# Causal masking of the first four query tiles' diagonal blocks: by TensorE in PSUM, or by ScalarE and GpSimd in SBUF

## The chip, the cores and the metric

The kernel runs on one core of one Trainium2 chip. The metric is the device time of one execution in microseconds, the median of several runs. Engines are named as in the profile: PE is TensorE (PEld its weight loads), DVE is VectorE, ACT is ScalarE, POOL is GpSimd, SP issues most DMAs.

## The reference

One transformer layer with adaptive modulation, in float32, on x of shape (16, 1024, 256):

```python
h = layernorm(x) * (1 + ca) + sa
x = x + ga * attn(h)        # attn: layer norm, Wq/Wk/Wv, rope, causal softmax, Wo; 16 heads of 16
h = layernorm(x) * (1 + cb) + sb
x = x + gb * moe_ffn(h)     # 8 experts, 512 tokens each, gathered and added back by index

scores = q @ k.T / 4        # attention, per batch and head
scores = scores * mask + (1 - mask) * -1e9      # mask: lower triangle
out = softmax(scores) @ v
```

The change lies in the attention alone. The exact maximum of each row of masked scores is taken there ahead of the exponentials.

## The kernel before, in words

Five phases follow each other: modulation vectors and weights (0), layer norms, q, k and v (1), attention (2), output projection (3) and the experts (4). The change is in phase 2. Its scores are products of bfloat16 parts: q and k are split into three parts each, six products of which are stacked on 96 rows, so that one pass gives a float32-like score.

A **unit** is one batch and one group of HG = 4 heads: 16 x 4 = 64 units. A row of 1024 queries is cut into T = 8 query tiles of 128. Each unit needs two passes over its scores:

- The pass for the **maxima** (`fill`, `largest`) has queries on the partitions. It goes through 20 slots (`SLOTS`, s0 to s19), each of two PSUM banks with up to 1024 score columns; even and odd slots take turns on two pairs of banks. TensorE fills a slot in two halves (`FILLS`, 40 of them), VectorE takes the row maxima of it in one reduction (line 946). Where a slot holds diagonal blocks, TensorE adds the causal mask by one more product of a unit matrix with `mask_b` (line 1034). Slot 4 (`TURN`) is kept free: there the finished maxima of the unit before are turned by TensorE (`turn_max`) and negated and split by VectorE (`negate`), then split on by GpSimd (`parts`) and sent by two DMAs of SP through DRAM (`maxima`) into rows 96 to 98 of q.
- The pass for the **exponentials** (`scores_for_exp`, `exp`, `weigh`) has keys on the partitions. It goes through NPC = 10 pieces of 4 heads each. For each head TensorE writes up to 512 columns into one of three banks (line 1052), with the negated maximum added by the three extra rows; ScalarE takes the exponential (line 992); GpSimd clears the upper triangle of diagonal blocks (line 885); two pieces later TensorE multiplies with v (`weigh`, line 1071). ScalarE copies the two halves of the output out of PSUM ahead of pieces 2 and 5 (`copy_out`, line 980).

Each engine's order is written out by hand. TensorE runs, for unit u and each of its 40 score matmuls n (piece n // 4, head n % 4), the score for the exponential and then fill n of unit u + 2; so piece i carries slots 2i and 2i + 1 of the unit two ahead. After four heads comes `weigh`. A fill of slot s waits until the slot s - 2, on the same banks, is reduced (line 1024); a score waits until the exponential three heads earlier is done (line 1050). VectorE goes through the slots in order. The last two units have nothing to fill ahead; the first two are filled in a prologue with no scores between.

Widths of the pieces: 0 has 512 columns a head, 1 has 384 + 128, 2 has 256, 3 to 7 have 512, 8 has 384 + 128, 9 has 256. Slots before: s0 has the diagonal blocks of tiles 0 and 4, s1 tile 1, s2 and s3 tile 2, s5 and s6 tile 3, s7 to s14 the first 512 columns of tiles 4 to 7, s15 to s19 the rest of tiles 5 to 7.

Of the kernel before, what the change touches and what calls it, by code (L numbers as in the profile page):

```python
# [17 lines left out]
F32 = mybir.dt.float32  # L18
# [3 lines left out]
ALU = mybir.AluOpType  # L22
ACT = mybir.ActivationFunctionType
AX = mybir.AxisListType
# [692 lines left out]
def phase2(nc, B, L, ps, ident, mask, q_d, k_d, v_d, max_d, att_d):  # L717
# [25 lines left out]
    both_banks = lambda i, k0, w: [[[(h, i, 0, k0, w)], [(h + 1, i, 0, k0, w)]] for h in range(0, HG, 2)]  # L743
    four = lambda i, k0: [(h, i, h * P, k0, P) for h in range(HG)]
    pairs = lambda i, k0: [[(h, i, (h % 2) * 256, k0, 256) for h in (n, n + 1)] for n in range(0, HG, 2)]
    SLOTS = [[four(0, 0), four(4, HALF)], pairs(1, 0)]
    for i in (2, 3):
        SLOTS += both_banks(i, 0, (i + 1) * P)
    for i in range(4, T):
        SLOTS += both_banks(i, 0, HALF)  # L750
    SLOTS += [pairs(5, HALF)]
    for i in (6, 7):
        SLOTS += both_banks(i, HALF, (i - 3) * P)
    TURN = 4
    SLOTS.insert(TURN, None)
    NS = len(SLOTS)
    NR = NS - 1
    real = lambda s: s - (s > TURN)
    FILLS = []
    for s, slot in enumerate(SLOTS):  # L760
        FILLS += [(s, 0), (s, 1)]
# [7 lines left out]
    with ExitStack() as ctx:  # L769
# [6 lines left out]
        prob = sb("prob", [P, RING, HG, 512], F32)  # L776
        unit_b = sb("unit_b", [P, P], BF16)
        mask_b = sb("mask_b", [P, P], BF16)
        mx = sb("mx", [P, 2, HG, T], F32)
        mx0 = sb("mx0", [P, 2, HG, 4], F32)  # L780
        m_rest = sb("m_rest", [HG * T, 2, P], F32)
# [1 line left out]
        o_sb = sb("o_sb", [P, 2, HALF], F32)  # L783

        qk_in, v_in, m_in = many("p2_qk_in", UNITS), many("p2_v_in", UNITS), many("p2_m_in", UNITS)
        ones_set, consts = sem("p2_ones_set"), sem("p2_consts")
        a_ready, a_free = sem("p2_a_ready"), sem("p2_a_free")
        turned = sem("p2_turned")
        max_done = sem("p2_max_done")
# [87 lines left out]
        @block.gpsimd  # L877
        def _(pool):
            def select(un, i):
                b, g, u = un  # L880

                wait_apart(pool, exp_done, u * NEXP + (i + 1) * HG)
                for _, at, _, _ in PIECES[i][1]:
                    own = prob[:, (g * NPC + i) % RING, :, at:at + P]
                    pool.affine_select(out=own, in_=own, compare_op=ALU.is_ge, fill=0.0, base=0,  # L885
                                       pattern=[[0, HG], [1, P]], channel_multiplier=-1).then_inc(sel_done, 1)

            def parts(un):

                b, g, u = un  # L890
                rest = m_rest[:, g % 2, :]
                wait_apart(pool, m_left, u + 1)
                pool.tensor_copy(m3[:, g % 2, 1, :], rest).then_inc(m_mid, 1)
                pool.wait_ge(m_mid, u + 1)
                pool.tensor_tensor(m3[:, g % 2, 2, :], rest, m3[:, g % 2, 1, :], ALU.subtract).then_inc(m_parts, 1)

            def step(un, ahead):
                for i in range(NPC):
                    if diag(PIECES[i]):
                        select(un, i)  # L900
                    if i == 3 and ahead is not None:
                        parts(prior(ahead))
                if ahead is None and un[1] == NG - AHEAD:
                    parts(unit(LAST, NG - 1))

            def prologue():
                for g in range(NG):
                    pool.memset(k[ROWS:P, g], 1.0).then_inc(ones_set, 1)
                parts(unit(0, 0))

            steps(pool, prologue, step)

        @block.vector
        def _(dve):
            def finish(un):
                b, g, u = un
                dve.wait_ge(a_free, u * NR + NR)
                late = mx[:, g % 2, :, 4:8]
                dve.tensor_tensor(late, late, mx0[:, g % 2], ALU.max).then_inc(max_done, 1)

            def negate(un):

                b, g, u = un
                hi, src = m3[:, g % 2, 0, :], ps[0:HG * T, PS_A + 2 * (TURN % 2), 0:P]
                dve.wait_ge(turned, u + 1)
                reuse(dve, m_saved, u * DMA - DMA)
                dve.tensor_scalar(hi, src, -1.0, None, ALU.mult).then_inc(m_hi, 1)
                dve.wait_ge(m_hi, u + 1)
                dve.scalar_tensor_tensor(m_rest[:, g % 2, :], src, -1.0, hi, ALU.mult, ALU.subtract).then_inc(m_left, 1)

            def largest(un, s):
                b, g, u = un
                at = PS_A + 2 * (s % 2)
                dve.wait_ge(a_ready, u * NR + real(s) + 1)
                (h, i, col, k0, w), per = SLOTS[s][0][0], len(SLOTS[s][0])
                m = mx[:, g % 2]
                if per == 4:
                    src = ps[:, at:at + 2, :].rearrange("p b (r n) -> p b r n", r=4)
                    dst = m[:, :, 0:8:4].rearrange("p h t -> p t h")
                elif per == 2:  # L940
                    src = ps[:, at:at + 2, :].rearrange("p b (r n) -> p (b r) n", r=2)
                    dst = m[:, :, i]
                else:
                    src = ps[:, at:at + 2, 0:w]
                    dst = mx0[:, g % 2, h:h + 2, i - 4] if i >= 4 and k0 == 0 else m[:, h:h + 2, i]
                dve.tensor_reduce(dst, src, AX.X, ALU.max).then_inc(a_free, 1)  # L946

            def whole(un, first=False):
                for s in range(NS):
                    if s == 2 and not first:  # L950
                        finish(prior(un))
                    if s != TURN:
                        largest(un, s)
                    elif not first:
                        negate(prior(un))

            def prologue():
                for n in range(AHEAD):
                    whole(unit(0, n), first=(n == 0))

            def step(un, ahead):
                if ahead is not None:
                    whole(ahead)
                elif un[1] == NG - AHEAD:
                    final = unit(LAST, NG - 1)
                    finish(final)
                    negate(final)

            dve.tensor_copy(unit_b[:, :], ident[:, :]).then_inc(consts, 1)
            dve.tensor_copy(mask_b[:, :], mask[:, 384:512]).then_inc(consts, 1)  # L970
            steps(dve, prologue, step)

        @block.scalar
        def _(act):
            def copy_out(un, c):
                b, g, u = un

                act.wait_ge(pv_done, u * NPC + (FIRST_HALF if c == 0 else NPC))
                reuse(act, o_stored[c], u * DMA)
                nc.scalar.copy(o_sb[:, c, :], ps[:, PS_O, :]).then_inc(o_copied, 1)  # L980

            def exp(un, i):
                b, g, u = un
                w = width(PIECES[i])
                for h in range(HG):
                    n = i * HG + h
                    act.wait_ge(b_ready, u * NEXP + n + 1)
                    if h == 0:

                        reuse(act, pv_done, u * NPC + i - RING + 1)  # L990
                    src = ps[:, PS_B + bank(g, n), 0:w]
                    nc.scalar.activation(prob[:, (g * NPC + i) % RING, h, 0:w], src, ACT.Exp).then_inc(exp_done, 1)  # L992

            def step(un, ahead, first=False):
                for i in range(NPC):
                    if i == LAG and not first:
                        copy_out(prior(un), 1)
                    if i == LAG + FIRST_HALF:
                        copy_out(un, 0)
                    exp(un, i)  # L1000

            for u in range(B * NG):
                step(unit(0, u), None, first=(u == 0))
            copy_out(unit(LAST, NG - 1), 1)

        @block.tensor
        def _(pe):
            def fill(un, n, first=False):
# [6 lines left out]
                    pe.wait_ge(qk_in[g], b * (DMA * NLD) + DMA * NLD)  # L1015
                if s == TURN:
                    if not first and half == 0:
                        pe.wait_ge(a_free, u * NR + s - 1)
                        turn_max(prior(un))
                    return  # L1020
                if half == 0 and s - 2 == TURN:
                    reuse(pe, m_left, u)
                elif half == 0:
                    reuse(pe, a_free, u * NR + (real(s - 2) + 1 if s >= 2 else s - 1))
                todo = SLOTS[s][half]
                for r, (h, i, col, k0, w) in enumerate(todo):
                    ins = pe.matmul(ps[:, at, col:col + w], q[0:ROWS, g, h, i * P:(i + 1) * P],  # L1027
                                    k[0:ROWS, g, h, k0:k0 + w], start=(r == 0), stop=True, skip_group_check=True)

                h, i, col, k0, w = todo[0]  # L1030
                if k0 + w == (i + 1) * P:
                    per = len(todo)
                    own = ps[:, at, :].rearrange("p (r n) -> p r n", r=per)[:, :, w - P:w]
                    ins = pe.matmul(own, unit_b[:, :], mask_b[:, :].rearrange("p (o n) -> p o n", o=1)  # L1034
                                    .to_broadcast([P, per, P]), start=False, stop=True, skip_group_check=True)
# [573 lines left out]
```

## Time and profile before

| | us |
|---|---|
| median of 3 runs | 3257.68 (3256.54 to 3258.6) |
| profiled execution: time | 3256.85 |
| profiled execution: span | 3255.1 |
| attention (phase 2) | from 763; the last unit begins at 2600 |
| one unit in its steady part | 28.20 |

A row of a timeline gives the start, the length from the first start to the last end of the merged instructions, engine, line, operation, operands and count, and in brackets the idle time ahead and what ended it. A matmul's length includes the way through the array: the distance of two starts is what TensorE needs for one. Steady units repeat every 28.20 us, so rows of neighbouring units can be set side by side.

### The profile page before, as it was taken

How to read it: one execution, taken by the hardware profiler on the slowest of the kernel's cores; microseconds unless marked ns; L12 is line 12 of the kernel's file. 1: busy time of each engine (PE TensorE's matmuls, PEld its weight loads, DVE VectorE, ACT ScalarE, POOL GpSimd, SP SyncE). 2: the span in 40 equal slices, each digit the busy share in tenths (PEclk: the TensorE clock that was granted, in tenths of full speed). 3: DMA queues.
4: the chain of work that ended last, by engine and by line, in shares of the span. 5: the costliest groups of instructions: out<-in, count | busy, mean ns of one | idle time of the engine just before them, and what ended most of it. 6: DMA issues, size and time to landing. Idle time of an engine off the chain costs nothing. (4 is left out here: it accounts for less than half of the span.)

```text
span 3255.1 us, 50330 instructions
## 1 busy us (share of the span) xinstructions
PE 2952.9 (91%) x18199; PEld 1403.3 (43%) x18199; DVE 2328.9 (72%) x3444; ACT 1713.4 (53%) x3591; POOL 1019.2 (31%) x1366
## 2 busy tenths in 40 slices
PE   2888998885999999999999999999999979975997
PEld 0444444441444444444444444444444347753664
DVE  5999999995777777777777777777777425543221
ACT  1444444430677777777777777777777731111111
POOL 3888888862122111112221111112221100003232
PEclk7999999996999999999999999999999989987999
DMA  2466666657244444444444444444444246663332
GB/s 77 138 180 191 191 191 191 184 156 175 55 95 93 95 100 100 100 96 92 94 95 92 97 100 100 100 96 90 95 92 92 48 173 259 259 230 110 78 100 56
DMA packets 175373, 403.11 MB, mean 124 GB/s; under 512 B 34556, under 2 KB 87202, under 8 KB 158518
## 3 DMA queue, kind: packets, MB, share of 16 engines
q1 hardware_dynamic: 168984, 391.37, 47.1%
q0 software_dynamic: 6144, 8.52, 1.5%
q8 instruction: 147, 2.41, 0.3%
q14 instruction: 98, 0.80, 0.1%
HBM read 240.65 MB, written 161.31 MB: 123 GB/s over the span
## 5 line engine op out<-in xcount | busy, mean ns | idle before, releaser
L946 DVE TENSOR_REDUCE mx<-ps 128x2 f32<-128x1024 f32 (+3 forms) x1216 | 1371.2, 1166 | 396.6 <-PE ps L1034 301.3
L992 ACT ACTIVATE prob<-ps 128x512 f32<-128x512 f32 (+1 forms) x2560 | 1251.4, 561 | 539.0 <-PE ps L1052 530.0
L1027 PE MATMUL ps<-k_rows,q_rows 96*128 96x512 bf16 (+3 forms) x3072 | 909.9, 332 | 40.6 <-DMA k_rows<-k_parts 33.1
L1052 PE MATMUL ps<-q_rows,k_rows 99*128 99x512 bf16 (+3 forms) x3072 | 908.5, 329 | 14.5 <-ACT prob L992 6.0
L885 POOL TENSOR_SCALAR_AFFINE_SELECT prob<-prob 128x512 f32<-128x512 f32 x512 | 318.6, 634 | 1453.8 <-ACT prob L992 1453.8
L1071 PE MATMUL ps<-prob,v_rows 128*32 128x512 f32 (+3 forms) x6144 | 628.6, 497 | 0.0
L1052 PEld LDWEIGHTS ps<-q_rows,k_rows 99*128 99x128 bf16 x3072 | 273.3, 98 | 598.8 <-ACT prob L992 359.8
L688 PE MATMUL ps<-w_all,x_t 128*128 128x512 f32 (+1 forms) x1024 | 427.9, 543 | 0.0
L1027 PEld LDWEIGHTS ps<-k_rows,q_rows 96*128 96x128 bf16 x3072 | 290.4, 98 | 269.8 <-DVE mx L946 60.4
L1034 PE MATMUL ps<-mask_b,unit_b 128*128 128x128 bf16 (+2 forms) x1408 | 348.5, 248 | 0.0
L1071 PEld LDWEIGHTS ps<-prob,v_rows 128*32 128x32 f32 x6144 | 134.7, 108 | 245.7 <-ACT prob L992 122.8
L688 PEld LDWEIGHTS ps<-w_all,x_t 128*128 128x128 f32 x1024 | 183.5, 200 | 125.4 <-issue 104.0
L481 DVE TENSOR_TENSOR qr<-m 128x256 f32<-128x256 f32 x256 | 224.2, 958 | 4.4
L641 POOL TENSOR_TENSOR stage<-rest,stage 128x512 bf16<-128x512 f32 x128 | 167.5, 1308 | 119.3 <-ACT stage L575 119.2
L1201 ACT COPY n_t<-ps 128x256 f32<-128x256 f32 x128 | 47.6, 372 | 232.7 <-PE ps L1223 232.7
L1469 DVE SCALAR_TENSOR_TENSOR y<-ps,gx,gate 128x256 f32<-128x256 f32 x32 | 15.5, 484 | 195.7 <-PE ps L1560 192.3
L1034 PEld LDWEIGHTS ps<-mask_b,unit_b 128*128 128x128 bf16 x1408 | 139.2, 99 | 22.8
L1235 PE MATMUL ps<-wg,n_t 128*128 128x256 f32 x512 | 145.7, 407 | 0.0
L561 ACT COPY v_st<-ps 128x256 f32<-128x256 f32 x128 | 47.7, 373 | 178.1 <-PE ps L688 178.1
L675 PE MATMUL ps<-ident,xn 128*128 128x128 f32 x256 | 55.9, 304 | 87.1 <-DVE xn L461 87.1
L1190 DVE TENSOR_TENSOR x<-ps,res_b 128x256 f32<-128x256 f32 x128 | 54.3, 425 | 106.2 <-PE ps L1235 106.2
L1560 PE MATMUL ps<-w,hid 128*128 128x256 f32 x512 | 119.1, 386 | 0.0
(143 smaller groups left out, 2707.4 us busy)
## 6 DMA issues: line engine op xcount, KB each, us to landing
k_rows<-k_parts SPq DMA_DIRECT2D x384, 128.0 KB, 7.5
v_ones<-v_st SPq DMA_DIRECT2D x64, 512.0 KB, 9.0
v_rows<-v_ones SPq DMA_DIRECT2D x64, 512.0 KB, 9.5
att<-o_sb SPq DMA_DIRECT2D x128, 256.0 KB, 3.2
att_b<-att SPq DMA_DIRECT2D x16, 2048.0 KB, 10.9
q_parts<-stage SPq DMA_DIRECT2D x192, 128.0 KB, 2.4
k_parts<-stage SPq DMA_DIRECT2D x192, 128.0 KB, 2.4
q_rows<-q_parts SPq DMA_DIRECT2D x64, 384.0 KB, 4.6
```

Source lines behind the costliest of these rows:

```text
L481: ins = dve.tensor_tensor(dst[:, :, :, :, e], src(m1)[:, :, :, :, e], src(m2)[:, :, :, :, 1 - e], ALU.add)
L641: pool.tensor_tensor(stage[:, p, 2, :, t * P:(t + 1) * P], rest[:, t % 2, :].rearrange("p (a n) -> p a n", a=4), stage[:, p, 1, :, t * P:( ...
L688: ins = pe.matmul(o, x_t[:, t % 2, k, :], w_all[:, k, lo:hi], start=False, stop=(k == KC - 1))
L885: pool.affine_select(out=own, in_=own, compare_op=ALU.is_ge, fill=0.0, base=0, pattern=[[0, HG], [1, P]], channel_multiplier=-1).then_inc( ...
L946: dve.tensor_reduce(dst, src, AX.X, ALU.max).then_inc(a_free, 1)
L992: nc.scalar.activation(prob[:, (g * NPC + i) % RING, h, 0:w], src, ACT.Exp).then_inc(exp_done, 1)
L1027: ins = pe.matmul(ps[:, at, col:col + w], q[0:ROWS, g, h, i * P:(i + 1) * P], k[0:ROWS, g, h, k0:k0 + w], start=(r == 0), stop=True, skip_ ...
L1034: ins = pe.matmul(own, unit_b[:, :], mask_b[:, :].rearrange("p (o n) -> p o n", o=1) .to_broadcast([P, per, P]), start=False, stop=True, s ...
L1052: ins = pe.matmul(ps[:, PS_B + bank(g, n), at:at + w], k[0:AUG, g, h, j * P:(j + 1) * P], q[0:AUG, g, h, q0:q0 + w], start=True, stop=True)
L1071: ins = pe.matmul(ps[32 * h:32 * h + 32, PS_O, col:col + w], v[:, g, j, h, :], prob[:, (g * NPC + i) % RING, h, at:at + w], start=(j == 0) ...
L1235: ins = pe.matmul(o, n_t[:, r % 2, k, :], wg[:, p, k, :], start=False, stop=(k == KC - 1))
L1560: ins = pe.matmul(o, hid[:, f, c * P:(c + 1) * P], w2[:, e % 2, f, :], start=False, stop=(f == FT - 1))
```

## The change

The blocks on the diagonal of tiles 0 to 3 leave the slots they shared with other columns. They get two slots of their own, `D_AT = (9, 19)`, each with two tiles of four heads; TensorE adds no mask there. ScalarE copies such a slot to SBUF (`take_own`, after the exponentials of pieces 4 and 9), GpSimd puts the masked value above the diagonal (`select_max`, one affine select over 8 x 128 columns), and VectorE takes the maxima from SBUF two slots later (`largest_own`, ahead of slots 11 and, for the unit after, 1) and joins them with the rest in `finish`. The banks of these two slots are free for TensorE when ScalarE has copied them. The order of the other slots follows: s0 has tile 1's first block and tile 4's diagonal, s1 tile 2, s2 and s3 tile 3, s5 to s8 and s10 to s13 the first 512 columns of tiles 4 to 7, s14 to s18 the rest of tiles 5 to 7.

```diff
-    SLOTS = [[four(0, 0), four(4, HALF)], pairs(1, 0)]
-    for i in (2, 3):
-        SLOTS += both_banks(i, 0, (i + 1) * P)
+    own = lambda i: four(i, i * P)
+    D_AT = (9, 19)
+    SLOTS = [[four(1, 0), four(4, HALF)], pairs(2, 0)] + both_banks(3, 0, 3 * P)
...
+    for n, s in enumerate(D_AT):
+        SLOTS.insert(s, [own(2 * n), own(2 * n + 1)])
...
+            def select_max(un, n):
+                b, g, u = un
+                wait_apart(pool, d_copied, u * ND + n + 1)
+                both = dg[:, n % 2].rearrange("p t h k -> p (t h) k")
+                pool.affine_select(out=both, in_=both, compare_op=ALU.is_ge, fill=MASKED, base=0,
+                                   pattern=[[0, 2 * HG], [-1, P]], channel_multiplier=1).then_inc(d_masked, 1)
...
                     if diag(PIECES[i]):
                         select(un, i)
+                    if ahead is not None and 2 * i + 1 in D_AT:
+                        select_max(ahead, D_AT.index(2 * i + 1))
...
-                parts(unit(0, 0))
+                pool.wait_ge(ones_set, NG)
+                for n in range(AHEAD):
+                    for d in range(ND):
+                        select_max(unit(0, n), d)
+                    if n == 1:
+                        parts(unit(0, 0))
...
+                dve.wait_ge(d_free, u * ND + ND)
+                dve.tensor_tensor(m[:, :, 0:4], m[:, :, 0:4], mxd[:, g % 2], ALU.max).then_inc(joined, 1)
+                dve.tensor_tensor(m[:, :, 4:8], m[:, :, 4:8], mx0[:, g % 2], ALU.max).then_inc(max_done, 1)
...
+            def largest_own(un, n):
+                b, g, u = un
+                dve.wait_ge(d_masked, u * ND + n + 1)
+                dst = mxd[:, g % 2, :, 2 * n:2 * n + 2].rearrange("p h t -> p t h")
+                dve.tensor_reduce(dst, dg[:, n % 2], AX.X, ALU.max).then_inc(d_free, 1)
+
             def whole(un, first=False):
                 for s in range(NS):
+                    if s - 2 in D_AT:
+                        largest_own(un, D_AT.index(s - 2))
+                    if s == 1 and not first:
+                        largest_own(prior(un), ND - 1)
...
+                    if s == TURN:
+                        dve.memset(mx[:, un[1] % 2, :, 0], MASKED).then_inc(low_set, 1)
...
+            def take_own(un, n):
+                b, g, u = un
+                act.wait_ge(a_ready, u * NA + ready(D_AT[n]))
+                reuse(act, d_free, u * ND + n - 1)
+                src = ps[:, PS_A + 2 * (D_AT[n] % 2):PS_A + 2 * (D_AT[n] % 2) + 2, :]
+                nc.scalar.copy(dg[:, n % 2].rearrange("p t h k -> p t (h k)"), src).then_inc(d_copied, 1)
...
                     exp(un, i)
+                    if ahead is not None and 2 * i + 1 in D_AT:
+                        take_own(ahead, D_AT.index(2 * i + 1))
...
+                elif half == 0 and s >= 2 and s - 2 in D_AT:
+                    pe.wait_ge(d_copied, u * ND + D_AT.index(s - 2) + 1)
...
-                if k0 + w == (i + 1) * P:
+                if k0 + w == (i + 1) * P and s not in D_AT:
```

## Rows read from the trace of the kernel before

**Rows 1.** The page: busy time of each engine; the group of the mask products.
```profile
PE 2952.9 (91%) x18199; PEld 1403.3 (43%) x18199; DVE 2328.9 (72%) x3444; ACT 1713.4 (53%) x3591; POOL 1019.2 (31%) x1366
...
L1034 PE MATMUL ps<-mask_b,unit_b 128*128 128x128 bf16 (+2 forms) x1408 | 348.5, 248 | 0.0
```

**Rows 2.** Stretches, one unit: busy time and count by engine, clock, DMA share, GB/s.
```profile
core 0: us, PE busy (x) PEld busy (x) DVE busy (x) ACT busy (x) POOL busy (x), PEclk, DMA share, GB/s
1494.96:1523.16 28.20, 28.14 (x219) 11.61 (x215) 22.00 (x23) 20.53 (x42) 5.62 (x11) 1.00 0.47 90
```

**Rows 3.** Groups by form, 1000 to 2500 us: busy, mean ns, idle before.
```profile
L992 ACT ACTIVATE prob<-ps 128x512 f32<-128x512 f32 x1702 | 894.2, 603 | 362.8 <-PE ps L1052 355.9
L946 DVE TENSOR_REDUCE mx<-ps 128x2 f32<-128x1024 f32 x639 | 758.3, 1222 | 210.6 <-PE ps L1034 129.4 <-PE ps L1027 78.0
...
L992 ACT ACTIVATE prob<-ps 128x256 f32<-128x256 f32 x427 | 146.9, 393 | 37.8 <-PE ps L1052 37.0
```

**Rows 4.** Timeline of TensorE: piece 5 begins at 1486.20, piece 6 at 1489.05.
```profile
1486.20 0.39 PE L1052 MATMUL ps<-q_rows,k_rows 99*128 99x512 bf16 x1
...
1487.52 0.38 PE L1052 MATMUL ps<-q_rows,k_rows 99*128 99x512 bf16 x1
...
1489.05 0.39 PE L1052 MATMUL ps<-q_rows,k_rows 99*128 99x512 bf16 x1
...
1490.15 0.38 PE L1027 MATMUL ps<-k_rows,q_rows 96*128 96x512 bf16 x1
```

**Rows 5.** Timeline of TensorE: pieces 0, 1 and 2 begin at 1500.49, 1504.02, 1506.47.
```profile
1500.49 0.39 PE L1052 MATMUL ps<-q_rows,k_rows 99*128 99x512 bf16 x1
...
1501.61 0.38 PE L1034 MATMUL ps<-mask_b,unit_b 128*128 128x512 bf16 x1
...
1504.02 0.39 PE L1052 MATMUL ps<-q_rows,k_rows 99*128 99x384 bf16 x2
...
1505.14 0.33 PE L1027 MATMUL ps<-k_rows,q_rows 96*128 96x384 bf16 x1
...
1506.47 0.28 PE L1052 MATMUL ps<-q_rows,k_rows 99*128 99x256 bf16 x1
...
1507.02 0.39 PE L1027 MATMUL ps<-k_rows,q_rows 96*128 96x512 bf16 x1
```

**Rows 6.** Timeline of VectorE in pieces 0 and 1: s0 and s1, then s2 and s3.
```profile
1502.02 2.36 DVE L946 TENSOR_REDUCE mx<-ps 128x8 f32<-128x1024 f32 x2 [0.84 <-PE ps L1034]
...
1505.12 1.85 DVE L946 TENSOR_REDUCE mx<-ps 128x2 f32<-128x768 f32 x2 [0.65 <-PE ps L1034]
```

**Rows 7.** Timeline of ScalarE: around piece 5, in piece 8, at piece 0.
```profile
1485.65 0.62 ACT L992 ACTIVATE prob<-ps 128x512 f32<-128x512 f32 x1
1486.33 0.58 ACT L980 COPY o_sb<-ps 128x512 f32<-128x512 f32 x1
1486.82 2.07 ACT L992 ACTIVATE prob<-ps 128x512 f32<-128x512 f32 x4
...
1495.39 2.06 ACT L992 ACTIVATE prob<-ps 128x512 f32<-128x512 f32 x4 [1.01 <-PE ps L1052]
...
1500.92 2.47 ACT L992 ACTIVATE prob<-ps 128x512 f32<-128x512 f32 x4 [1.21 <-PE ps L1052]
```

**Rows 8.** Groups by form, whole span: VectorE's reduction out of SBUF.
```profile
L1432 DVE TENSOR_REDUCE again<-twice 128x4 f32<-128x512 f32 x8 | 5.5, 686 | 0.3
```

**Rows 9.** Timeline of GpSimd: the two selects of piece 8.
```profile
1497.59 1.22 POOL L885 TENSOR_SCALAR_AFFINE_SELECT prob<-prob 128x512 f32<-128x512 f32 x2 [2.44 <-ACT prob L992]
```

**Rows 10.** Timeline, the start of the first unit and of the last.
```profile
806.42 0.42 POOL L895 TENSOR_TENSOR m<-m_rest,m 32x128 bf16<-32x128 f32 x1
...
808.48 0.24 SPq L843 DMA_DIRECT2D q_rows<-neg_max  x1
...
823.23 0.63 PE L1052 MATMUL ps<-q_rows,k_rows 99*128 99x512 bf16 x1
...
2597.98 0.25 SPq L843 DMA_DIRECT2D q_rows<-neg_max  x1
...
2600.12 1.91 PE L1052 MATMUL ps<-q_rows,k_rows 99*128 99x512 bf16 x4 [4.62 <-DMA q_rows<-neg_max]
```

More of the change, by code:

```diff
@@ L745, in phase2 @@
     pairs = lambda i, k0: [[(h, i, (h % 2) * 256, k0, 256) for h in (n, n + 1)] for n in range(0, HG, 2)]
-    SLOTS = [[four(0, 0), four(4, HALF)], pairs(1, 0)]
-    for i in (2, 3):
-        SLOTS += both_banks(i, 0, (i + 1) * P)
+    own = lambda i: four(i, i * P)
+    D_AT = (9, 19)
+    ND = len(D_AT)
+    TURN = 4
+    SLOTS = [[four(1, 0), four(4, HALF)], pairs(2, 0)] + both_banks(3, 0, 3 * P)
     for i in range(4, T):
@@ L753, in phase2 @@
         SLOTS += both_banks(i, HALF, (i - 3) * P)
-    TURN = 4
     SLOTS.insert(TURN, None)
+    for n, s in enumerate(D_AT):
+        SLOTS.insert(s, [own(2 * n), own(2 * n + 1)])
     NS = len(SLOTS)
-    NR = NS - 1
-    real = lambda s: s - (s > TURN)
+    NA = NS - 1
+    NR = NA - ND
+    ready = lambda s: s + 1 - (s > TURN)
+    taken = lambda s: ready(s) - sum(d < s for d in D_AT)
     FILLS = []
@@ L778, in phase2 @@
         mask_b = sb("mask_b", [P, P], BF16)
+        dg = sb("dg", [P, 2, 2, HG, P], F32)
+        mxd = sb("mxd", [P, 2, HG, 4], F32)
         mx = sb("mx", [P, 2, HG, T], F32)
@@ L785, in phase2 @@
         qk_in, v_in, m_in = many("p2_qk_in", UNITS), many("p2_v_in", UNITS), many("p2_m_in", UNITS)
-        ones_set, consts = sem("p2_ones_set"), sem("p2_consts")
+        ones_set, low_set, consts = sem("p2_ones_set"), sem("p2_low_set"), sem("p2_consts")
+        d_copied, d_masked, d_free, joined = sem("p2_d_copied"), sem("p2_d_masked"), sem("p2_d_free"), sem("p2_joined")
         a_ready, a_free = sem("p2_a_ready"), sem("p2_a_free")
@@ L916, in finish @@
                 b, g, u = un
+                m = mx[:, g % 2]
                 dve.wait_ge(a_free, u * NR + NR)
-                late = mx[:, g % 2, :, 4:8]
-                dve.tensor_tensor(late, late, mx0[:, g % 2], ALU.max).then_inc(max_done, 1)
+                dve.wait_ge(d_free, u * ND + ND)
+                dve.tensor_tensor(m[:, :, 0:4], m[:, :, 0:4], mxd[:, g % 2], ALU.max).then_inc(joined, 1)
+                dve.tensor_tensor(m[:, :, 4:8], m[:, :, 4:8], mx0[:, g % 2], ALU.max).then_inc(max_done, 1)
             def negate(un):
@@ L933, in largest @@
                 at = PS_A + 2 * (s % 2)
-                dve.wait_ge(a_ready, u * NR + real(s) + 1)
+                dve.wait_ge(a_ready, u * NA + ready(s))
                 (h, i, col, k0, w), per = SLOTS[s][0][0], len(SLOTS[s][0])
@@ L938, in largest @@
                     src = ps[:, at:at + 2, :].rearrange("p b (r n) -> p b r n", r=4)
-                    dst = m[:, :, 0:8:4].rearrange("p h t -> p t h")
+                    dst = m[:, :, 1:5:3].rearrange("p h t -> p t h")
                 elif per == 2:
@@ L946, in largest @@
                 dve.tensor_reduce(dst, src, AX.X, ALU.max).then_inc(a_free, 1)
+            def largest_own(un, n):
[3 more added lines that the diff above has]
+                dve.tensor_reduce(dst, dg[:, n % 2], AX.X, ALU.max).then_inc(d_free, 1)
             def whole(un, first=False):
                 for s in range(NS):
+                    if s - 2 in D_AT:
+                        largest_own(un, D_AT.index(s - 2))
+                    if s == 1 and not first:
+                        largest_own(prior(un), ND - 1)
                     if s == 2 and not first:
                         finish(prior(un))
-                    if s != TURN:
+                    if s == TURN:
+                        dve.memset(mx[:, un[1] % 2, :, 0], MASKED).then_inc(low_set, 1)
+                        if not first:
+                            negate(prior(un))
+                    elif s not in D_AT:
                         largest(un, s)
-                    elif not first:
-                        negate(prior(un))
             def prologue():
@@ L965, in step @@
                     final = unit(LAST, NG - 1)
+                    largest_own(final, ND - 1)
                     finish(final)
@@ L992, in exp, with step @@
                     nc.scalar.activation(prob[:, (g * NPC + i) % RING, h, 0:w], src, ACT.Exp).then_inc(exp_done, 1)
-            def step(un, ahead, first=False):
+            def step(un, ahead):
                 for i in range(NPC):
-                    if i == LAG and not first:
+                    if i == LAG and un[2]:
                         copy_out(prior(un), 1)
@@ L1000, in step, with prologue @@
                     exp(un, i)
-            for u in range(B * NG):
-                step(unit(0, u), None, first=(u == 0))
+                    if ahead is not None and 2 * i + 1 in D_AT:
+                        take_own(ahead, D_AT.index(2 * i + 1))
+            def prologue():
+                for n in range(AHEAD):
+                    for d in range(ND):
+                        take_own(unit(0, n), d)
+            steps(act, prologue, step)
             copy_out(unit(LAST, NG - 1), 1)
@@ L1017, in fill @@
                     if not first and half == 0:
-                        pe.wait_ge(a_free, u * NR + s - 1)
+                        pe.wait_ge(a_free, u * NR + taken(s - 2))
                         turn_max(prior(un))
@@ L1022, in fill @@
                     reuse(pe, m_left, u)
+                elif half == 0 and s >= 2 and s - 2 in D_AT:
+                    pe.wait_ge(d_copied, u * ND + D_AT.index(s - 2) + 1)
+                elif half == 0 and s >= 2:
+                    pe.wait_ge(a_free, u * NR + taken(s - 2))
+                elif half == 0 and s - 2 + NS in D_AT:
+                    reuse(pe, d_copied, u * ND - ND + D_AT.index(s - 2 + NS) + 1)
                 elif half == 0:
-                    reuse(pe, a_free, u * NR + (real(s - 2) + 1 if s >= 2 else s - 1))
+                    reuse(pe, a_free, u * NR - NR + taken(s - 2 + NS))
                 todo = SLOTS[s][half]
```

## The prediction

> **What bounds the kernel now.** I read the page's totals first, then the stretches, then the timeline of single engines over one unit. TensorE is busy for 91% of the span [rows 1]. In the attention stage one unit takes 28.20 us and TensorE is busy for 28.14 of it, at a granted clock of 1.00; VectorE has 22.00, ScalarE 20.53, GpSimd 5.62 [rows 2]. So in that stage each column that TensorE no longer pushes is time saved, unless another engine then makes it wait. The shares say that VectorE and ScalarE have room (6 and 8 us a unit), but only on average. What counts is the order in which work reaches them, and the timelines show that both stand close behind TensorE in two places: before the first fill of s3 (piece 1) and before the last head's scores of piece 5.
>
> **What is removed.** Of 22 mask products a unit (1408 in 64 units [rows 1]) 11 go: the four diagonal blocks of tiles 0 to 3, 4 x 512 = 2048 columns. Matmuls of 512 columns follow each other at (1487.52 - 1486.20) / 6 = 0.22 us [rows 4], so this is 4 x 0.22 = 0.87 us a unit. The score columns for the maxima stay at 18432 a unit; 12 more matmuls carry them in smaller pieces, at the same pace (in s0 four of 128 columns take the 0.22 us of one of 512: the mask product at 1501.61 stands 1.12 us, five such steps, behind the start of the piece [rows 5]). By piece, since the slots move: piece 0 loses two products of 512 (0.44), piece 1 four of 128 (0.22), pieces 2, 3 and 9 two of 128 each (0.11), piece 8 gains 0.11, piece 7 is even. Only 62 of the 64 steps fill anything ahead.
>
> **What is added on VectorE, and where it is late.** It still does 19 large reductions a unit, 15 of 1024 elements and 4 of 768, but two of them, of the blocks masked in SBUF, are now done a piece later than their slot was filled. Slot 19 is filled in piece 9, so in piece 0 VectorE has three reductions in a row: s0, the masked pair, s1 (largest_own stands ahead of s1). From the start of piece 0:
> - s0 is ready at 1502.02 - 1500.49 = 1.53 [rows 5, 6], less one mask product ahead of it, 1.31.
> - Two reductions take 2.36, one 1.22 [rows 3, 6], so the next one starts 1.14 behind the last. s1 ends at 1.31 + 2 x 1.14 + 1.22 = 4.81; TensorE runs 0.05 later (1505.12 + 1.85 = 1506.97, then 1507.02 [rows 5, 6]): 4.86.
> - The third fill of piece 1 (s3, the same banks as s1) now starts 1504.02 - 1500.49 = 3.53 and 1505.14 - 1504.02 = 1.12 in [rows 5]. Without the masks ahead of it: 3.09 + 1.01 = 4.10.
>
> TensorE waits 4.86 - 4.10 = 0.76 us in piece 1, where it waits for nothing now. The masked pair itself isn't late: the copy fits into ScalarE's gap of 1.21 us ahead of piece 0 [rows 7], and the select is done some 0.8 us before VectorE comes to it. In piece 2 s5 waits for s3 already (to 1507.02), and s3 will be later; of the 0.11 there I keep 0.05.
>
> How long a reduction out of SBUF is: the nearest row is 686 ns for 512 elements [rows 8], against 1222 for 1024 out of PSUM; 536 ns for 512 elements more leave the source no difference to speak of. I take 1.22; the ends are 1.37 (twice 686) and 1.10, a tenth less. The Trainium skill, VectorE: DVE Perf Modes, section on the TRN2 errata, gives VectorE a fixed part of 58 cycles for a source in SBUF and 120 in PSUM, which is an estimated 65 ns less for each of the two new reductions. The two rows would then differ by about 600 ns and not 536, so the trace does not bear it out; by the page the time would be about 8 us lower.
>
> **What is added on ScalarE, and where it is late.** Two copies of 1024 columns a unit. The trace has none of that size. A 256 exponential takes 0.39, a 512 one 0.60 [rows 3], so 512 columns more are 0.42, on top of the 0.49 at which a copy of 512 lets the next start (1486.33 to 1486.82 [rows 7]): 0.91, and 1.00 to its end. The ends are 0.49 and 0.98 (none and all of a second copy). From the start of piece 5 (1486.20):
> - The last exponential of piece 4 starts at -0.55 (1485.65) and lets go at -0.06. The copy of slot 9 takes -0.06 to 0.85, the old copy of the output 0.85 to 1.34. The first exponential of piece 5 starts at 1.34; now at 0.62.
> - It ends 0.60 later, and TensorE, with three banks for these scores, needs that for its fourth head: 1.34 + 0.60 + 0.05 = 1.99. Now TensorE is there at 1.32 [rows 4], with 0.05 to spare. It waits 0.67 us.
> - VectorE follows. The copy is whole at 0.94; GpSimd starts 0.14 behind ScalarE (1495.39 + 2.06 = 1497.45, then 1497.59) and takes 1.22, as two selects of 512 do [rows 7, 9]; VectorE starts on it at 2.35 and s11, behind it, ends at 2.35 + 1.14 + 1.22 = 4.71. The third fill of piece 6 needs it: 2.85 + 0.67 + (1490.15 - 1489.05) = 4.62 against 4.76 [rows 4]. It waits 0.14 us more.
>
> The two belong together: without ScalarE's delay TensorE would be at that fill at 3.95 and wait 0.81 there. So pieces 5 and 6 cost 0.81 unless both chains are shorter. A select between 0.63 (one of 512) and 1.26 (two apart) puts this between 0.67 and 0.85. After piece 9 the other copy delays nothing, since piece 0 has no old copy in front. Small operations (a memset, one more maximum of 16 elements) lie where VectorE runs ahead of the transposed maxima: nothing, or 0.1 if that cover is gone.
>
> **The sum for a unit.** Saved 0.44 + 0.22 + 0.05 + 0.11 + 0.11 = 0.93, less 0.11 in piece 8: 0.82. Lost 0.76 + 0.81 = 1.57. Net +0.75, times 62: +46 us.
>
> **Once, at the start.** On GpSimd parts() of the first unit now stands behind four masking steps, the last of which waits for slot 19 of the second unit. Now it ends at 806.84, long before the first scores at 823.23 [rows 10]. It will come behind a copy (0.4 and 1.0), a select (0.14 and 1.22) and its own 0.8, and SP's two DMAs wait behind it: 808.48 - 806.84 = 1.64 to the second, and 2600.12 - 2597.98 = 2.14 until TensorE has the rows. That is 7.3 us behind the last fill; with the fills ending about as now and a slow restart of TensorE I take +8, between 4 and 12. The last two units change by less than 1 us.
>
> Against the profiled execution of 3256.85 us (its span is 3255.1; the median of the runs is 0.8 higher): 3256.85 + 46 + 8 = **3311 us**.
>
> **The rivals.**
> 1. Not slower: the room shown by the shares takes in all of it, and only the mask products are felt: 3256.85 - 62 x 0.87 + 8 = 3211. For it: VectorE idles 22% and ScalarE 27% of a unit. Against it: the idle time lies in other places. It decides in piece 0, where s0, the masked pair and s1 would have to be done 0.05 ahead of the fill at 4.10, so within 4.05 - 1.31 = 2.74 us, 0.91 each, against 1.14 by the rows. Chance 0.12.
> 2. One of the two delays doesn't come. Without that of piece 1 the time is 3311 - 47 = 3264, without those of pieces 5 and 6 3311 - 50 = 3261. For it: each hangs on gaps of a few tenths between rows. Against it: each has about 0.7 to lose. Chance 0.10, half of it within the bound of no change.
> 3. GpSimd's select over 1024 elements takes twice what I take. VectorE then comes to the masked pair of slot 9 1.2 us later, and all of it falls on piece 6: 3311 + 62 x 1.2 = 3385. Against it: two selects of 512 follow each other at 0.59. Chance 0.06.
>
> That the change doesn't take out the products would show as 1408 of them, and not 11 x 64 = 704; the condition in fill() leaves no room for that.
>
> **How the numbers follow.** The forecast holds 0.72. Inside it the net of a unit lies between 0.5 and 1.1 (a reduction 0.1 up or down, the copy at 0.8 to 0.98, the select), so 3256.85 + 31 + 4 = 3292 to 3256.85 + 68 + 12 = 3337. To hold 8 of 10 I let the range reach towards rival 2: 3275 to 3340. A difference under 0.2% (6.5 us) can't be told from none: faster 0.12 (rival 1), the same 0.05, slower 0.83.
>
> **What would show it.** In a unit of the changed kernel: a period of 28.9 to 29.0; 11 mask products; TensorE's fill of s3 released by VectorE's reduction with 0.6 to 0.9 idle, and the fourth scores of piece 5 released by ScalarE with about as much; ScalarE copies of 128x1024 of about 1.0 us, one of them directly ahead of the output copy; three reductions without a gap in pieces 0 and 5; the first exponential about 7 us later. A period below 28.2, with TensorE's fills never waiting for VectorE in piece 1, would make the forecast wrong.

## The result, and the profile after

The changed kernel takes 3314.2 us (median of 4 runs, 3312.1 to 3315.3) against 3258.1 before (4 runs, 3256.5 to 3259.2): a ratio of 1.0172, 95% interval 1.0154 to 1.0189. It is slower, by more than the runs scatter, and 3 us from the forecast. The profiled execution has a span of 3312.9 us, 57.8 more than before. Half of the 1408 mask products are gone, as the prediction had it:
```profile
L1093 PE MATMUL ps<-mask_b,unit_b 128*128 128x128 bf16 (+2 forms) x704 | 174.5, 248 | 0.0
```

The stretch of one unit, against [rows 2]; columns as there (length, then busy time and count of TensorE, its weight loads, VectorE, ScalarE and GpSimd, granted clock, DMA share, GB/s):
```profile
1528.80:1557.71 28.91, 27.72 (x217) 11.36 (x216) 22.08 (x25) 22.26 (x44) 7.83 (x13) 1.00 0.45 94
```
A unit is 28.91 us instead of 28.20, at the same clock. TensorE's busy time fell by 0.42 us, and 1.2 us of every unit are now idle, where 0.06 were. (A matmul of 512 columns counts as busy for 0.38 us where the next can start after 0.22. So a delay of 0.76 by the pace shows as an idle time of 0.60, the rest counts as busy, and the busy time falls by less than the products cost.)

Who waited for whom from 1000 to 2500 us, some 52 units (engine, line, what it waited for: us in total, times, longest). L1086 are the fills, L1111 the scores, L971 the reductions, L1039 the exponentials; PEld rows are the weight loads ahead of the matmuls:
```profile
PEld ps L1086 <- DVE mx L971: 83.5, 156, 0.9
PE ps L1086 <- DVE mx L971: 31.6, 53, 0.6
PE ps L1111 <- ACT prob L1039: 27.0, 51, 0.5
...
DVE mxd L978 <- POOL dg L910: 0.3, 1, 0.3
```
The two PE rows are the idle of the array itself, once a unit each: a fill that waits for VectorE (0.6) and a score that waits for ScalarE (0.5). VectorE waits for GpSimd's masked data once in 1500 us, for 0.3.

VectorE in pieces 0 to 2 (piece 0 begins at 1531.03), against [rows 6]:
```profile
1532.35 1.23 DVE L971 TENSOR_REDUCE mx<-ps 128x8 f32<-128x1024 f32 x1 [1.65 <-PE ps L1093]
1533.48 1.21 DVE L978 TENSOR_REDUCE mxd<-dg 128x8 f32<-128x1024 f32 x1
1534.61 1.22 DVE L971 TENSOR_REDUCE mx<-ps 128x4 f32<-128x1024 f32 x1
...
1535.91 1.82 DVE L971 TENSOR_REDUCE mx<-ps 128x2 f32<-128x768 f32 x2
```
TensorE in piece 1, against [rows 5]:
```profile
1534.12 0.39 PE L1111 MATMUL ps<-q_rows,k_rows 99*128 99x384 bf16 x2
...
1534.90 0.38 PE L1111 MATMUL ps<-q_rows,k_rows 99*128 99x384 bf16 x2
1535.89 0.34 PE L1086 MATMUL ps<-k_rows,q_rows 96*128 96x384 bf16 x1 [0.60 <-DVE mx L971]
```
s0, the masked pair and s1 stand in a row, 1.13 us apart. s1 ends at 1534.61 + 1.22 = 1535.83, and the fill of s3 starts 0.06 later; by the pace of the piece (1.01 behind its start, as predicted) it would have stood at 1535.13. That is 0.76 us.

ScalarE around piece 5 (which begins at 1544.88), against [rows 7], and TensorE there, against [rows 4]:
```profile
1542.88 2.07 ACT L1039 ACTIVATE prob<-ps 128x512 f32<-128x512 f32 x4 [0.78 <-PE ps L1111]
1544.80 1.04 ACT L1027 COPY dg<-ps 128x1024 f32<-128x1024 f32 x1
1545.70 0.64 ACT L1019 COPY o_sb<-ps 128x512 f32<-128x512 f32 x1
1546.17 2.13 ACT L1039 ACTIVATE prob<-ps 128x512 f32<-128x512 f32 x4
```
```profile
1544.88 0.39 PE L1111 MATMUL ps<-q_rows,k_rows 99*128 99x512 bf16 x1
...
1546.89 0.39 PE L1111 MATMUL ps<-q_rows,k_rows 99*128 99x512 bf16 x1 [0.53 <-ACT prob L1039]
...
1548.43 0.39 PE L1111 MATMUL ps<-q_rows,k_rows 99*128 99x512 bf16 x1
...
1551.33 0.39 PE L1111 MATMUL ps<-q_rows,k_rows 99*128 99x512 bf16 x1
```
The new copy lets go after 0.90 and is followed at once by the output copy. The first exponential starts 1.29 behind the start of the piece, 0.62 before; the fourth head's scores stand at 2.01, 1.32 before. Piece 5 (to 1548.43) takes 3.55 us instead of 2.85, piece 6 (to 1551.33) 2.90 instead of 2.84. VectorE has three reductions in a row there too: s10, the masked pair, s11.
```profile
1545.96 1.23 DVE L971 TENSOR_REDUCE mx<-ps 128x2 f32<-128x1024 f32 x1 [1.21 <-PE ps L1086]
1547.17 1.22 DVE L978 TENSOR_REDUCE mxd<-dg 128x8 f32<-128x1024 f32 x1
1548.30 3.57 DVE L971 TENSOR_REDUCE mx<-ps 128x2 f32<-128x1024 f32 x3
```
The pair starts 1.21 behind s10, where reductions without a gap start 1.13 apart: the masked data come late by less than 0.1 us. (That does not show as a wait, since s10's reduction counts as busy until then.)

The start of the first unit, against [rows 10]:
```profile
833.76 0.58 PE L1111 MATMUL ps<-q_rows,k_rows 99*128 99x512 bf16 x1 [7.04 <-DMA q_rows<-neg_max]
```
The first scores come 10.5 us later than before, 7.04 of it idle. Then the clock: in these stretches of 8 us (the granted clock is the third column from the end; 0.50 is 1.2 GHz, 1.00 is 2.4) it stays at half until about 846:
```profile
834.00:842.00 8.00, 7.80 (x34) 3.99 (x33) 5.60 (x9) 5.54 (x11) 1.31 (x3) 0.50 0.00 1
842.00:850.00 8.00, 8.00 (x45) 2.52 (x46) 4.27 (x6) 3.83 (x9) 1.83 (x4) 0.71 0.03 6
850.00:858.00 8.00, 7.47 (x51) 2.33 (x49) 6.79 (x6) 6.62 (x14) 1.09 (x1) 1.00 0.10 36
```
Before, it was back sooner:
```profile
824.00:832.00 8.00, 7.51 (x51) 3.71 (x49) 6.18 (x9) 5.58 (x12) 2.30 (x4) 0.87 0.00 1
832.00:840.00 8.00, 8.00 (x62) 2.90 (x58) 6.58 (x7) 6.41 (x13) 0.83 (x3) 1.00 0.11 39
```
From its first score to the start of its piece 4 the first unit takes 14.83 us (833.76 to 848.59), before 11.95 (823.23 to 835.18). With the 10.5 us this is some 13.5 us lost at the start.

The sum of 62 x 0.71 = 44 us and some 13.5 us at the start makes up the 57.8 of the span, but for 0.3.

### The profile page after: what moved, and what is told of

It is laid out like the page before. It is cut to its first block and busy times, and to the rows that moved or that the text cites. A ratio compares the mean times of both kernels' runs of the same rounds, so it can differ in the third digit from the quotient of the medians.

```text
span 3312.9 us, 51288 instructions
## 1 busy us (share of the span) xinstructions
PE 2929.3 (88%) x18263; PEld 1389.0 (42%) x18263; DVE 2334.1 (70%) x3572; ACT 1825.5 (55%) x3719; POOL 1161.0 (35%) x1494
## 5 line engine op out<-in xcount | busy, mean ns | idle before, releaser
L971 DVE TENSOR_REDUCE mx<-ps 128x2 f32<-128x1024 f32 (+3 forms) x1088 | 1239.2, 1160 | 448.8 <-PE ps L1093 259.4
L1039 ACT ACTIVATE prob<-ps 128x512 f32<-128x512 f32 (+1 forms) x2560 | 1256.5, 566 | 424.3 <-PE ps L1111 422.1
L1086 PE MATMUL ps<-k_rows,q_rows 96*128 96x128 bf16 (+3 forms) x3840 | 911.4, 300 | 85.3 <-DVE mx L971 47.1
L1111 PE MATMUL ps<-q_rows,k_rows 99*128 99x512 bf16 (+3 forms) x3072 | 911.1, 330 | 50.9 <-ACT prob L1039 38.9
L1111 PEld LDWEIGHTS ps<-q_rows,k_rows 99*128 99x128 bf16 x3072 | 281.2, 98 | 620.9 <-ACT prob L1039 408.2
L1086 PEld LDWEIGHTS ps<-k_rows,q_rows 96*128 96x128 bf16 x3840 | 344.8, 99 | 346.0 <-DVE mx L971 128.9
L910 POOL TENSOR_SCALAR_AFFINE_SELECT dg<-dg 128x1024 f32<-128x1024 f32 x128 | 140.0, 1094 | 416.2 <-ACT dg L1027 416.2
L1027 ACT COPY dg<-ps 128x1024 f32<-128x1024 f32 x128 | 131.1, 1024 | 78.9 <-PE ps L1086 78.9
L1093 PE MATMUL ps<-mask_b,unit_b 128*128 128x128 bf16 (+2 forms) x704 | 174.5, 248 | 0.0
L978 DVE TENSOR_REDUCE mxd<-dg 128x8 f32<-128x1024 f32 x128 | 155.7, 1216 | 2.1 <-POOL dg L910 2.1
```

The source lines that it names most:

```text
L978: dve.tensor_reduce(dst, dg[:, n % 2], AX.X, ALU.max).then_inc(d_free, 1)
L1111: ins = pe.matmul(ps[:, PS_B + bank(g, n), at:at + w], k[0:AUG, g, h, j * P:(j + 1) * P], q[0:AUG, g, h, q0:q0 + w], start=True, stop=True)
```

## The experiments

Each is the changed kernel with one edit, but for e4, which is the kernel before with one. Times are medians; the kernel before ran beside them at 3257.0 to 3257.6.

**e4: what the mask products cost.** On the kernel before, whose row maxima of tiles 0 to 3 then go over unmasked scores:
```diff
-                if k0 + w == (i + 1) * P:
+                if k0 + w == (i + 1) * P and i >= 4:
```


> The kernel before, with TensorE's mask products of the diagonal blocks of tiles 0 to 3 left out and nothing in their place (the row maxima of these tiles then go over unmasked scores as well). It measures what the removed products cost by themselves. My theory (TensorE is the bound, 2048 columns at 0.22 us for 512 are 0.87 us a unit): 62 x 0.87 = 54 us less than before, 3204; period 27.3 to 27.4. Rival (the mask products are hidden anyway, behind VectorE's reductions or the weight loads): less than 20 us, 3240 or more.

3207.5 us, ratio 0.9848 (0.9831 to 0.9864); a unit takes 27.40:
```profile
1507.87:1535.27 27.40, 27.30 (x205) 10.88 (x204) 21.95 (x22) 20.25 (x43) 5.63 (x11) 1.00 0.48 99
```
So the products do cost nearly what their columns say (0.87), 0.80 us a unit and 50 us in all, and the changed kernel, which has 704 products too, saves that. What it takes above this run, 107 us, is paid elsewhere: 62 x (28.91 - 27.40) = 94 us in the units, and the rest, 13, is about what the start costs.

**e2: the order of the pair and s1.**
```diff
-                    if s == 1 and not first:
-                        largest_own(prior(un), ND - 1)
                     if s == 2 and not first:
+                        largest_own(prior(un), ND - 1)
                         finish(prior(un))
```


> The changed kernel, with VectorE's reduction of the second masked pair moved from ahead of s1 to behind it (still ahead of finish()). My theory (in pieces 0 to 2 VectorE has one reduction too many, whatever its order, because s5 needs all of s0, the pair, s1, s2 and s3 done): the 0.76 us wait ahead of s3's fill in piece 1 goes, and about as much comes back ahead of the turned maxima and s5's fill in piece 2; the period stays at 28.8 to 29.0 and the time within 6 us of 3314. Rival (the order alone is the cause: the pair stands in front of s1, whose banks are wanted): the period falls by 0.76 us to 28.15 and the time by 47 us to 3267.

3316.6 us, period 28.94. TensorE in pieces 1 and 2, and VectorE's s2 and s3:
```profile
1536.19 0.33 PE L1085 MATMUL ps<-k_rows,q_rows 96*128 96x384 bf16 x1
...
1537.80 0.28 PE L1100 MATMUL ps<-ident,mx 128*32 128x128 f32 x1 [0.50 <-DVE mx L971]
...
1538.67 0.39 PE L1085 MATMUL ps<-k_rows,q_rows 96*128 96x512 bf16 x1 [0.36 <-ACT prob L1038]
```
```profile
1536.79 1.82 DVE L971 TENSOR_REDUCE mx<-ps 128x2 f32<-128x768 f32 x2
```
s3's fill no longer waits. The turning of the maxima and s5's fill do instead. (The last row names ScalarE, but a fill waits for no exponential; the reduction of s3 ends at 1538.61, 0.06 before this fill.) Piece 1 takes 2.22 us instead of 2.99, piece 2 3.29 instead of 2.49: as much comes back one piece later. The order is not the cause; the number of reductions between s0 and s5 is.

**e7: shorter reductions of the pairs.** Half of each block's columns is left out of its maxima:
```diff
-                dve.tensor_reduce(dst, dg[:, n % 2], AX.X, ALU.max).then_inc(d_free, 1)
+                dve.tensor_reduce(dst, dg[:, n % 2, :, :, 0:P // 2], AX.X, ALU.max).then_inc(d_free, 1)
```


> The changed kernel, with VectorE's two reductions of the pairs cut to half of each block's columns (512 of 1024 elements; the other half of these maxima is left out). Copies and selects stay whole. My theory (piece 1 waits for three reductions in a row): each is 0.53 us shorter; the wait ahead of s3's fill in piece 1 falls from 0.76 to about 0.23, piece 6's 0.05 goes, piece 5's wait for ScalarE stays; 0.53 to 0.68 us a unit less: 3272 to 3281. Rival (it isn't VectorE's time but the wait for the masked data that delays the order): no change, 3310 or more.

3273.5 us, period 28.33: 0.58 us a unit for reductions of 683 ns instead of 1216. s3's fill stands 0.24 behind its pace, where it stood 0.76:
```profile
1516.19 0.38 PE L1111 MATMUL ps<-q_rows,k_rows 99*128 99x384 bf16 x2
1516.65 0.34 PE L1086 MATMUL ps<-k_rows,q_rows 96*128 96x384 bf16 x1
```
Piece 1's wait is VectorE's own time, not the arrival of the masked data. Piece 6's 0.06 goes as well (2.85 us), and the wait for ScalarE in piece 5 stays at 0.53.

**e6: half of the copy ahead of piece 5.**
```diff
+                dst = dg[:, n % 2].rearrange("p t h k -> p t (h k)")
+                if n == 0:
+                    src, dst = src[:, 0:1, :], dst[:, 0:1, :]
-                nc.scalar.copy(dg[:, n % 2].rearrange("p t h k -> p t (h k)"), src).then_inc(d_copied, 1)
+                nc.scalar.copy(dst, src).then_inc(d_copied, 1)
```
(GpSimd sets the other half once, in the prologue; the maxima of tile 1's block are left out.)


> The changed kernel, with ScalarE's copy of the first pair (slot 9) cut to half, 512 of 1024 columns; the other half of the buffer keeps a constant, so the maxima of tile 1's diagonal block are left out. GpSimd's select and VectorE's reduction stay whole. My theory (pieces 5 and 6 are bound by two chains of about the same length, ScalarE's and VectorE's): the wait for ScalarE in piece 5 falls from 0.6-0.7 to 0.2-0.25 us, and the wait for VectorE at s13's fill in piece 6 grows from 0.05 to 0.4-0.5; time 3305 to 3314. Rival (ScalarE alone makes piece 5 late): 0.42 us a unit less, 3288.

3310.1 us, period 28.86. TensorE from piece 5 (1515.39) to piece 7 (1521.76):
```profile
1515.39 0.39 PE L1117 MATMUL ps<-q_rows,k_rows 99*128 99x512 bf16 x1
...
1516.97 0.39 PE L1117 MATMUL ps<-q_rows,k_rows 99*128 99x512 bf16 x1
...
1518.51 0.39 PE L1117 MATMUL ps<-q_rows,k_rows 99*128 99x512 bf16 x1
...
1520.01 0.39 PE L1092 MATMUL ps<-k_rows,q_rows 96*128 96x512 bf16 x1 [0.24 <-DVE mx L974]
...
1521.76 0.39 PE L1117 MATMUL ps<-q_rows,k_rows 99*128 99x512 bf16 x1
```
The fourth head of piece 5 stands at 1.58 instead of 2.01, but s13's fill in piece 6 now stands 1.50 behind the piece's start, 1.10 by its pace. Pieces 5 and 6 together take 6.37 us, 6.45 in the changed kernel, 5.69 before. Of the 0.43 us by which the fourth head comes sooner, 0.08 arrives: two chains of nearly the same length lie there, and shortening one of them gives the time to the other. The second is VectorE's own, as in piece 1:
```profile
1516.47 1.23 DVE L974 TENSOR_REDUCE mx<-ps 128x2 f32<-128x1024 f32 x1 [1.21 <-PE ps L1092]
1517.61 1.21 DVE L981 TENSOR_REDUCE mxd<-dg 128x8 f32<-128x1024 f32 x1
1518.73 3.48 DVE L974 TENSOR_REDUCE mx<-ps 128x2 f32<-128x1024 f32 x3
```
With the masked data there early, the pair starts 1.14 behind s10 and can't start sooner. So in pieces 5 and 6 an earlier copy or select could gain no more than this 0.08.

**e3: the first pair elsewhere.**
```diff
-    D_AT = (9, 19)
+    D_AT = (13, 19)
...
-                    if s - 2 in D_AT:
-                        largest_own(un, D_AT.index(s - 2))
+                    if s - 3 in D_AT:
+                        largest_own(un, D_AT.index(s - 3))
```


> The changed kernel, with the first pair's slot at 13 instead of 9, so that its copy lies behind piece 6 and no output copy follows it, and with VectorE's reduction of it three slots later (ahead of s16). The second pair stays at 19. My theory (the copy and the output copy stand in one gap of ScalarE and make the fourth head of piece 5 wait 0.6 to 0.7 us): the waits of pieces 5 and 6 go, 0.65 to 0.75 us a unit, so 40 to 46 us less: 3268 to 3274. Rival (two copies, two selects and two reductions more are simply too much for ScalarE, GpSimd or the SBUF, wherever they stand): the waits show up around piece 7, 3310 to 3318.

3264.6 us, ratio 1.0023 (1.0013 to 1.0032) to before; period 28.16. ScalarE and VectorE are busy for nearly as long as in the changed kernel (22.26 and 22.08):
```profile
1506.80:1534.96 28.16, 27.49 (x217) 11.48 (x216) 21.82 (x25) 22.23 (x44) 7.82 (x13) 1.00 0.46 95
```
The waits of pieces 5 and 6 are gone, 0.75 us of 0.76, and none came up at piece 7. The load isn't too high; its place was wrong. The edit moves the copy and the pair's reduction together, so it does not tell what each alone would give.

The time lies 3 us below the range that was expected. The units give 62 x 0.75 = 46.5 of the 49.6 us, the rest lies at the start: the first scores come 1.3 us sooner, and the clock rises sooner though TensorE stood idle nearly as long:
```profile
832.45 0.58 PE L1111 MATMUL ps<-q_rows,k_rows 99*128 99x512 bf16 x1 [6.94 <-DMA q_rows<-neg_max]
```
```profile
832.00:840.00 8.00, 6.56 (x33) 3.56 (x33) 5.22 (x7) 5.05 (x10) 1.00 (x2) 0.70 0.00 1
```

**e1: the start.**
```diff
                 for n in range(AHEAD):
+                    if n == 1:
+                        parts(unit(0, 0))
                     for d in range(ND):
                         select_max(unit(0, n), d)
-                    if n == 1:
-                        parts(unit(0, 0))
```


> The changed kernel, with GpSimd's parts() of the first unit moved ahead of the two masking steps of the second unit in the prologue; nothing else. My theory (the first scores wait for parts(), which waits for the last masking step of the prologue): the wait of 7.0 us ahead of the first score goes, and with it part of the slow restart of TensorE's clock, so 7 to 10 us less than the changed kernel: about 3305. Rival (the start is late because VectorE waits for the masked pairs in the prologue): no change, 3314. The steady period of a unit stays at 28.91 us under both.

3305.8 us; the period stays at 28.91. The first scores stand at 827.01 instead of 833.76, directly behind the last fill, and the clock is back at 1.00 from 836 on:
```profile
828.00:836.00 8.00, 7.58 (x36) 3.56 (x37) 5.96 (x10) 7.07 (x14) 2.95 (x4) 0.59 0.00 1
836.00:844.00 8.00, 7.72 (x61) 2.94 (x60) 5.49 (x5) 6.06 (x12) 1.88 (x4) 1.00 0.02 6
```
Of some 13.5 us lost at the start 8.4 come back.

**e5: both pairs elsewhere, and the start.** The edit of e1, the later reductions of e3, and:
```diff
-    D_AT = (9, 19)
+    D_AT = (13, 15)
...
-                    if s == 1 and not first:
-                        largest_own(prior(un), ND - 1)
```
(also without the last `largest_own(final, ND - 1)`, since the pair is now reduced in its own unit).


> The changed kernel with both pairs' slots moved, to 13 and 15, the reductions of the pairs three slots later (ahead of s16 and s18, in the same unit), and parts() of the first unit ahead of the second unit's masking steps, as in e1. My theory (the change's work fits if it stands where ScalarE has a wide gap, pieces 6 to 8, and VectorE its shorter reductions, and is done before s0): nothing waits in a unit but piece 2's s5, as before; the saving of 0.82 to 0.87 us a unit is left: period 27.3 to 27.45 us, time 3258 - 52 + 4 = 3205 to 3215, faster than before. Rival (two more copies and reductions cost something wherever they stand): more than 3240.

3209.6 us, ratio to before 0.9852 (0.9836 to 0.9869), a unit of 27.43 us: faster than both kernels by 1.5% and 3.2%, and 2 us from e4, which has no masking of these blocks at all. Three things are changed at once here; e3 and e1 show what two of them give, and the rest, from a period of 28.16 to 27.43, goes with the second pair's move. ScalarE and VectorE in pieces 6 to 9 (piece 7 begins at 1504.49, piece 8 at 1507.58):
```profile
1503.98 1.05 ACT L1024 COPY dg<-ps 128x1024 f32<-128x1024 f32 x1
1504.92 2.19 ACT L1036 ACTIVATE prob<-ps 128x512 f32<-128x512 f32 x4
1506.99 1.02 ACT L1024 COPY dg<-ps 128x1024 f32<-128x1024 f32 x1
1508.01 2.06 ACT L1036 ACTIVATE prob<-ps 128x512 f32<-128x512 f32 x4
```
```profile
1506.94 1.21 DVE L978 TENSOR_REDUCE mxd<-dg 128x8 f32<-128x1024 f32 x1
1508.67 1.85 DVE L971 TENSOR_REDUCE mx<-ps 128x2 f32<-128x768 f32 x2 [0.52 <-PE ps L1090]
1510.44 1.21 DVE L978 TENSOR_REDUCE mxd<-dg 128x8 f32<-128x1024 f32 x1
```
No output copy stands behind these copies: the first exponentials of pieces 7 and 8 start 0.43 behind the piece's start, in piece 8 just as before the change (1494.96 to 1495.39 in [rows 2, 7]). Each pair's reduction is done before s0 comes. In 1500 us TensorE is idle for 5.

## Why the prediction was right

- **The saving.** Worked out as 0.82 us a unit, with 0.05 of piece 2 counted; e4 measures 0.80 for the same blocks in the old order of slots. Right; the mask products are not hidden by anything.
- **Piece 1, VectorE late by three reductions.** 0.76 predicted, 0.76 measured; e7 and e2 show that it is the work and neither the order nor the data. The reduction from SBUF takes 1216 ns, those from PSUM 1222 to 1226. By the Trainium skill (VectorE: DVE Perf Modes, the section on the TRN2 errata) the one from SBUF would be an estimated 65 ns shorter; this trace has 6 to 10 and does not bear that out, as [rows 8] did not.
- **Pieces 5 and 6.** 0.67 and 0.14 predicted, 0.70 and 0.06 measured: 0.81 against 0.76. The copy lets go after 0.90 (0.91). The term that was off is GpSimd's select, 1.09 us where I had 1.22 from two selects of 512; part of it is lost again, as the select starts 1.16 behind the piece's start (1546.04) where I had 1.08. VectorE starts on the pair at 2.29 instead of 2.35, and piece 6 waits less. That the two waits belong together, which the prediction gave as 0.81 "at that fill" without ScalarE's delay, is what e6 shows from its side. But the prediction hung VectorE's chain on the copy and the select alone; by e6 the reduction of s10 in front would hold the pair back to 2.22 without them.
- **The period.** +0.75 predicted, +0.71 measured, 46 and 44 us.
- **The start** is the mis-sized term: +8 with an end at 12, measured about 13.5. The chain itself was right (7.3 from the last fill to the first score; 826.55 to 833.76 is 7.2). Wrong was "the fills ending about as now": they end at about 826.6 and not 823.2. The first fill already begins 0.8 later (775.89 against 775.12); it begins between 775.1 and 777.9 in the runs here, so this part is within their scatter. In each of the prologue's two units VectorE has to wait 1.1 us ahead of s10, as slot 9 goes to ScalarE first, and comes to the pair between s10 and s11 while TensorE stands idle:
```profile
814.75 1.23 DVE L971 TENSOR_REDUCE mx<-ps 128x2 f32<-128x1024 f32 x1 [1.13 <-PE ps L1086]
```
And the slow restart was taken for less than a microsecond (8 less 7.3); the rows of the clock put it at 2.9. How long it lasts is not set by the idle time alone, by e3; what sets it was not shown. e1 gives back the wait and part of the restart. The rest of the start was not taken apart further.
- **The rivals.** The first ("the room shown by the shares takes in all of it") fails for this kernel: in piece 0 the three reductions do start 1.13 apart. Its sum, 3211 us, is close to what e5 takes (3209.6), with the same work in other places and the start of e1. The second fails, both delays came. In the third the select would have been twice as long as taken; it was shorter.

By luck the two errors partly cancel: 2 us too much in the units, 5.5 too little at the start. That the forecast is within 3 us is in part this.

## What to carry to other kernels

Work that is moved from the bounding engine to idle ones is free only where the idle time lies: write out, for the piece in which each moved instruction lands, what stands in front of it and who waits behind it, and compare with the buffers' depth. Where two chains end at nearly the same time, taking time off one of them gives little (e6, 0.08 us), and a move that takes both out of that place gives nearly all (e3, 0.75). A kernel that came out slower can hold a faster one: here the same instructions in other slots turn +1.7% into -1.5%.

## What the runs showed of the hardware

GpSimd's select over 128 x 1024 in place took 1094 ns, two over 128 x 512 (strided) 1.23 us together and 637 ns each, so the larger one was the cheaper per element; whether by its size or because it is contiguous is not shown. ScalarE's copy of 1024 columns across two banks took 1012 ns (median) and let the next start after 0.90. After TensorE had stood idle for 7.04 us behind a stretch at the half clock (1.2 GHz), the granted clock stayed at 0.50 from 834 to 842, while TensorE was busy for 7.80 of these 8 us, and rose to 1.00 (2.4 GHz) at about 846. Without that idle time (e1) it was 0.59 from 828 to 836 and 1.00 after that. With 6.94 us of idle time (e3) it had 0.70 from 832 to 840: it rose some 4 us after the first score, not 12. So the same idle time came with very different ends of the half clock.
